# A decayed scan interleaved over chunks, with one gathered reciprocal a chunk, and shorter bias loading one layer later

## What is computed

```python
q = _phi(to_bhtd(q)); k = _phi(to_bhtd(k)); v = to_bhtd(v)   # _phi(x) = elu(x) + 1
kv = k * v
run_kv_f, kv_f1 = _decay_scan(kv, log_a, z)
run_ks_f, ks_f1 = _decay_scan(k, log_a, z)
...
den_f = jnp.clip(jnp.sum(q * run_ks_f, axis=-1, keepdims=True), eps, None)
out_f = (q * run_kv_f / den_f).transpose(0, 2, 1, 3).reshape(B, T, HID)
...
out = jnp.concatenate([out_f, out_s], axis=-1) @ w_out
```

## Time and profile before

| | us |
|---|---|
| median of 3 runs | 3821.74 (3816.81 to 3832.23) |
| the profiled execution, its own time | 3824.2 |
| its span | 3822.5 |
| PE, DVE, ACT, POOL busy | 3128.6, 1936.0, 1324.9, 1112.3 |
| scan stage, from its first DMA to the next stage's | 1841.0 to 2111.1 |
| start of layer 2's attention, its first DMA | 2675.2 |

### The profile page before, as it was taken

The page is one execution under the profiler, slowest core; times in us unless marked ns, Lnnn a source line. Parts: engine busy times, 40 slices in busy tenths (PEclk is TensorE's granted clock), DMA queues, the critical chain, the costliest instruction groups (busy, mean ns, idle before and its releaser), DMA issues. The chain is left out here.

```text
span 3822.5 us, 46802 instructions
## 1 busy us (share of the span) xinstructions
PE 3128.6 (82%) x17066; PEld 1946.8 (51%) x17066; DVE 1936.0 (51%) x3143; ACT 1324.9 (35%) x2216; POOL 1112.3 (29%) x946
## 2 busy tenths in 40 slices
PE   6769999999999899999554874998585667788776
PEld 3445555555555378888322562666463444233354
DVE  3365565565666542332567751111358737466574
ACT  2224444444444343332100541332233414244542
POOL 0015666666666600000111313111342202011231
PEclk9879999999999999999676886999797868589987
DMA  3010000000000011120000134222101000000000
GB/s 105 0 47 1 1 1 1 1 1 1 1 1 1 8 55 50 34 61 28 15 0 0 32 124 134 33 34 43 19 2 30 6 8 2 0 1 1 1 26 25
DMA packets 110925, 89.20 MB, mean 23 GB/s; under 512 B 20451, under 2 KB 104189, under 8 KB 110717
## 3 DMA queue, kind: packets, MB, share of 16 engines
q1 hardware_dynamic: 101501, 75.73, 6.6%
q0 software_dynamic: 7152, 8.55, 1.3%
q10 hardware_dynamic: 2064, 2.10, 0.2%
HBM read 68.32 MB, written 18.94 MB: 23 GB/s over the span
## 5 line engine op out<-in xcount | busy, mean ns | idle before, releaser
L684 POOL TENSOR_TENSOR acc<-acc,pf 128x512 f32<-128x512 f32 (+1 forms) x448 | 563.8, 1280 | 254.4 <-ACT pf L811 254.4
L868 DVE TENSOR_REDUCE mxa<-ps 128x1 f32<-128x512 f32 x512 | 327.3, 681 | 229.2 <-PE ps L730 227.3
L811 ACT ACTIVATE pf<-ps 128x512 f32<-128x512 f32 x512 | 278.0, 595 | 318.7 <-PE ps L705 293.9
L718 PE MATMUL ps<-pf,v 128*64 128x512 f32 (+1 forms) x1152 | 311.0, 618 | 0.0
L3206 DVE TENSOR_REDUCE mx<-ps 128x2 f32<-128x1024 f32 (+1 forms) x192 | 184.0, 958 | 146.7 <-PE ps L3100 108.4
L3194 ACT ACTIVATE pT<-ps 128x1024 f32<-128x1024 f32 (+1 forms) x192 | 153.3, 811 | 207.5 <-PE ps L3112 207.1
L730 PE MATMUL ps<-kH,qH 64*128 64x512 f32 x512 | 158.0, 443 | 23.9 <-DVE mc L876 18.6
L1518 POOL TENSOR_TENSOR e<-e,sm 128x1232 f32<-128x1232 f32 x48 | 107.9, 2248 | 221.6 <-DVE sm L1773 221.6
L1065 POOL TENSOR_TENSOR x<-x,ys 128x256 f32<-128x256 f32 x16 | 11.8, 740 | 508.4 <-DVE ys L1270 508.4
L3096 PE MATMUL ps<-kT,qT 64*128 64x512 f32 (+2 forms) x384 | 98.9, 511 | 66.8 <-DVE mx L3206 59.5
L2165 DVE TENSOR_SCALAR ys<-ps,xs 128x256 f32<-128x256 f32 x39 | 18.8, 483 | 251.4 <-PE ps L2021 251.4
(11 more groups left out here) (498 smaller groups left out, 7169.9 us busy)
## 6 DMA issues: line engine op xcount, KB each, us to landing
w_raw<-in_c_h SPq DMA_DIRECT2D x32, 512.0 KB, 3.8
w1a<-in_f_w SPq DMA_DIRECT2D x8, 1024.0 KB, 15.1
w2a<-in_f_w SPq DMA_DIRECT2D x8, 1024.0 KB, 13.1
moe_rows<-pad SPq DMA_DIRECT2D x1, 5167.5 KB, 19.7
xs<-moe_rows SPq DMA_DIRECT2D x39, 132.5 KB, 2.1
w_raw<-in_c_w SPq DMA_DIRECT2D x32, 128.0 KB, 2.3
x<-in_x SPq DMA_DIRECT2D x1, 2048.0 KB, 8.3
moe_acc<-x ACTq DMA_DIRECT2D x1, 2048.0 KB, 21.1
```

Of the source, the lines that this page charges most:

```text
L684: pool.tensor_tensor(now[0:r, :], now[0:r, :], pf[0:r, n % RING, a, :], ALU.add).then_inc(added.sem, 1)
L718: ins = pe.matmul(g.bk(3)[SIDE[a], :], v[0:r, u // 2 % 2, t, u % 2 * P + a * HD:u % 2 * P + (a + 1) * HD], pf[0:r, n % RING, a, :], start= ...
L811: act.activation(pf[0:r, n % RING, a, :], g.bk(bk.bank[f"s{n}_{a}"])[0:r, :], ACT.Exp, bias=bias)\
L868: dve.tensor_reduce(mxa[:, q % 2, half, a, j:j + 1], g.bk(4 + a), AXX, ALU.max).then_inc(bk.release(f"m{q}_{i}_{a}"), 1)
```

## The change

**Scan stage.** The loops are written out, and the work of three neighbouring chunks is interleaved. PE turns and projects chunk c+1 while DVE scans chunk c and finishes chunk c-1. Features, v and the scans have two buffers each; a scan starts from the last column of the other buffer. The normalisation is part of the block, with z made on ACT (scale `rstd`, shift -mean * rstd). ACT also takes max(x, 0) (`pos`) and copies v out of PSUM, and DVE makes a feature from the two in one pass. The kv product on POOL and the qk product on DVE stay where they were. Denominators are gathered: `summed` has one column per head, 32 for both sets, and four groups of 32 PSUM partitions take the four token tiles, so that one 128x128 tile of bank 4 holds every denominator of a chunk. DVE clamps and inverts this tile alone; PE spreads the inverses back over the features with `spread_back` (16 products a chunk) and DVE multiplies `num` by them, one token tile at a time.

**Layer 2's attention.** The biases come as two rows (`brow`), ACT packs them, four one-column products turn them, ACT copies them to `bcol`. Weights of q and k have a semaphore of their own, and PE starts on them; the wait for the rest comes later.

```diff
@@ -1276,128 +1276,289 @@
...
+        summed, spread_back = sb("summed", [P, NI, 32]), sb("spread_back", [P, NI, P])
...
+        kx, qx, pos = sb("kx", [P, 2, KD, CH]), sb("qx", [P, 2, KD, CH]), sb("pos", [P, 2, KD, CH])
+        v, kv = sb("v", [P, 2, KD, CH]), sb("kv", [P, KD, CH])
+        run_k, run_kv = sb("run_k", [P, 2, NI, CH]), sb("run_kv", [P, 2, NI, CH])
+        qk, num, rec = sb("qk", [P, NI, CH]), sb("num", [P, 2, NI, CH]), sb("rec", [P, P])
...
+            fills += [(f"t0_{c}", 0), (f"t1_{c}", 1), (f"k0_{c}", 2), (f"v0_{c}", 3), (f"q0_{c}", 0), (f"k1_{c}", 1), (f"v1_{c}", 2), (f"q1_{c}", 3)]
+            fills += [(f"d_{c}", 4)] + [(f"b{j}_{c}", 4 + j) for j in range(TC)] + [(f"y{j}_{c}", 4 + j) for j in range(TC)]
...
+                def denominators(c):
+
+                    pe.wait_ge(*bk.free(f"d_{c}", 0))
+                    for n, i in enumerate(ORDER):
+                        pe.wait_ge(*qk_made.at(0, at_scan(i, c)))
+                        for j in range(TC):
+                            ins = pe.matmul(g.bk(4)[32 * j:32 * j + 32, 0:P], summed[:, i, :], qk[:, i, j * P:(j + 1) * P], start=n == 0, stop=n == NI - 1)
+                    ins.then_inc(bk.fill(f"d_{c}"), 1)
+
+                def reciprocals_back(c):
+                    pe.wait_ge(*rec_made.at(0, c + 1))
...
+                        pe.wait_ge(*bk.free(f"b{j}_{c}", 0))
+                    for i in range(NI):
+                        for j in range(TC):
+                            r = slice(32 * j, 32 * j + 32)
+                            ins = pe.matmul(g.bk(4 + j)[:, i * P:(i + 1) * P], spread_back[r, i, :], rec[r, :], start=True, stop=True)
...
+                for c in range(-1, NC + 1):
+                    if 0 <= c - 1:
+                        denominators(c - 1)
+                    if c + 1 < NC:
+                        for n, f in [("t", 0), ("t", 1)] + BLOCKS[0:3]:
+                            if (n, f) == BLOCKS[0]:
+                                pe.wait_ge(*wq_in.at(0, 16))
+                            project(n, f, c + 1)
+                    if 0 <= c - 1:
+                        reciprocals_back(c - 1)
+                    if c + 1 < NC:
+                        for n, f in BLOCKS[3:6]:
+                            project(n, f, c + 1)
+                    if 0 <= c - 1:
+                        output(c - 1)
...
+                    act.activation((kx if n == "k" else qx)[:, h, f, :], src, ACT.Exp).then_inc(ex_made.sem, 1)
+                    act.activation(pos[:, f, n == "q", :], src, ACT.Relu).then_inc(pos_made.sem, 1)
+                    act.wait_ge(*ex_made.at(0, m))
+                    act.wait_ge(*pos_made.at(0, m))
+                    act.sem_inc(bk.release(name), 1)
...
+                for c in range(NC):
+                    for k in range(KD):
+                        act.wait_ge(*bk.full(f"t{k}_{c}", 0))
+                        if c:
+                            act.wait_ge(*bk.full(f"q1_{c - 1}", 0))
+                        act.activation(zT[:, k, :], g.bk(bk.bank[f"t{k}_{c}"]), ACT.Copy).then_inc(bk.release(f"t{k}_{c}"), 1)
+                    if c + 1 < NC:
+                        normalised(c + 1)
+                    for n, f in BLOCKS:
+                        features(n, f, c)
...
+                        pool.wait_ge(*kv_run.at(0, at_scan(i, c)))
+                        if c >= 2:
+                            pool.wait_ge(*bk.full(f"y{TC - 1}_{c - 2}", 0))
+                        pool.tensor_tensor(num[:, h, i, :], qx[:, h, f, :], run_kv[:, h, i, :], ALU.mult).then_inc(num_made.sem, 1)
...
+                    dve.scalar_tensor_tensor(dst, dst, 1.0, pos[:, f, n == "q", :], ALU.min, ALU.add).then_inc(phi.sem, 1)
...
+                    for run, src, made, used in ((run_k, kx[:, h, f, :], k_run, qk_made), (run_kv, kv[:, f, :], kv_run, num_made)):
+                        if c >= 2:
+                            dve.wait_ge(*used.at(0, at_scan(i, c - 2)))
+                        if made is kv_run:
+                            dve.wait_ge(*kv_made.at(0, KD * c + f + 1))
+                        first = none[:, 0:1]
+                        if c % NB:
+                            dve.wait_ge(*made.at(0, at_scan(i, c - 1)))
+                            first = run[:, 1 - h, i, CH - 1:CH]
+                        dve.tensor_tensor_scan(run[:, h, i, :], d, src, first, ALU.mult, ALU.add).then_inc(made.sem, 1)
...
+                    dve.tensor_tensor(qk[:, i, :], qx[:, h, f, :], run_k[:, h, i, :], ALU.mult).then_inc(qk_made.sem, 1)
...
+                    dve.tensor_scalar(rec[:], g.bk(4)[:, 0:P], 1e-6, None, ALU.max).then_inc(bk.release(f"d_{c}"), 1)
+                    dve.wait_ge(*bk.read(f"d_{c}", 0))
+                    dve.reciprocal(rec[:], rec[:]).then_inc(rec_made.sem, 1)
...
+                        dst = num[:, c % 2, :, j * P:(j + 1) * P]
+                        dve.tensor_tensor(dst, dst, g.bk(4 + j).rearrange("p (i n) -> p i n", n=P), ALU.mult).then_inc(y_made.sem, 1)
+                        dve.wait_ge(*y_made.at(0, TC * c + j + 1))
+                        dve.sem_inc(bk.release(f"b{j}_{c}"), 1)
...
+                for c in range(NC + 1):
+                    if c < NC:
+                        made_feature("k", 0, c)
+                        made_feature("q", 0, c)
+                        key_values(0, c)
+                        scans(0, c)
+                        scans(2, c)
+                    if c:
+                        inverted(c - 1)
+                    if c < NC:
+                        made_feature("k", 1, c)
+                        made_feature("q", 1, c)
+                        key_values(1, c)
+                    if c:
+                        divided(c - 1)
+                    if c < NC:
+                        scans(1, c)
+                        scans(3, c)
+                    if c:
+                        added(c - 1)
...
@@ -2254,18 +2417,14 @@
         with nc.Block() as block:
             @block.sync
             def _(sp):
-                for h in range(NH):
-                    f, r = divmod(h, G)
-                    for i, src in enumerate((bk_, bq)):
-                        sp.dma_start(bcol[h % NB * HD:h % NB * HD + HD, 2 * i + h // NB:2 * i + h // NB + 1], src[32 * r:32 * r + HD, f:f + 1],
-                                     allow_slow_non_contiguous=True).then_inc(w_in.sem, 16)
+                for i, src in enumerate((bk_, bq)):
+                    sp.dma_start(brow[0:1, i, :].rearrange("o (f p) -> o f p", p=P), src.rearrange("p f -> f p").unsqueeze(0), allow_slow_non_contiguous=True)\
+                        .then_inc(b_in.sem, 16)
                 for dst, src in ((wk, Wk), (wq, Wq)):
                     for k in range(KD):
                         sp.dma_start(dst[:, k].rearrange("p (h d) -> p h d", d=HD),
-                                     rows(src)[:, k].rearrange("p (h e) -> p h e", e=2 * HD)[:, :, 0:HD]).then_inc(w_in.sem, 16)
-                for dst, src in ((wv, Wv), (wo, Wo)):
-                    load(sp, dst[:], rows(src), w_in)
-                for dst, src in ((rv, bv), (ro, bo), (cau, causal), (same, same_head)):
+                                     rows(src)[:, k].rearrange("p (h e) -> p h e", e=2 * HD)[:, :, 0:HD]).then_inc(kq_in.sem, 16)
+                for dst, src in ((same, same_head), (cau, causal), (wv, rows(Wv)), (rv, bv), (wo, rows(Wo)), (ro, bo)):
...
@@ -2406,11 +2565,16 @@
                         ins = pe.matmul(g.bk(bk.bank[f"w{t}"])[:, 0:D], oT[:, k, :], wo[:, k, :], start=k == 0, stop=k == KD - 1)
                     ins.then_inc(bk.fill(f"w{t}"), 1)
 
+                pe.wait_ge(*bias_dense.at(0, 1))
+                for m in range(2 * KD):
+                    ins = pe.matmul(g.bk(0)[:, m:m + 1], bdense[0:1, m // KD, m % KD * P:(m % KD + 1) * P], g.ident[0:1, 0:1], start=True, stop=True)
+                ins.then_inc(bk.fill("bias"), 1)
+                pe.wait_ge(*kq_in.at(0, 64))
+                for p in start:
+                    project(*p)
                 pe.wait_ge(*made.at(0, 2))
                 pe.wait_ge(*emptied.at(0, 3))
-                pe.wait_ge(*w_in.at(0, 16 * (10 + 2 * NH)))
-                for p in start:
-                    project(*p)
+                pe.wait_ge(*w_in.at(0, 96))
...
+                act.wait_ge(*b_in.at(0, 32))
+                act.activation(bdense[:].rearrange("o i (h d) -> o i h d", d=HD), brow[:].rearrange("o i (h e) -> o i h e", e=2 * HD)[:, :, :, 0:HD], ACT.Copy)\
+                    .then_inc(bias_dense.sem, 1)
+                act.wait_ge(*bk.full("bias", 0))
+                act.activation(bcol[:], g.bk(0)[:, 0:2 * KD], ACT.Copy).then_inc(bk.release("bias"), 1)
+                act.wait_ge(*bk.read("bias", 0))
```

More of the change, by code:

```diff
@@ L1304, in _ @@
             @block.tensor
             def _(pe):
[L1306 to L1314, removed]
-                        for k in range(KD):
[L1316 to L1322, removed]
```

(33 more changed lines are left out.)

216 lines of the change are left out of this document (129 added, 87 removed).

## The result

The changed kernel takes 3684.82 us (median of 4 runs, 3681.95 to 3691.5) where the kernel before takes 3821.18 (4 runs of the same comparison, 3816.81 to 3832.23). The ratio is 0.9641, 95% interval 0.9616 to 0.9667. The forecast was 3665 with a range of 3641 to 3700: the time lies inside it, 20 us above the point.

The account below looks back on a forecast made before the run. The prediction took the scan stage as a DVE-PE chain and layer 2's attention as waiting on SP's DMA queue. Savings of 139.6 and 18.1 us from 3824.2 gave 3666.5, 3665 against the runs' median; range 3641 to 3700.

Parts of the forecast that it names:

- three periods: Scan stage: chunks 1 to 3 each take one period of the fullest queue, DVE, at 25.4 us.
- the 21.8: Scan stage: DVE's own passes, scans, products, denominators and sums in one period, 21.8 us before POOL's effect.
- POOL's charge: Scan stage: DVE loses 0.88 us for each of four POOL products, 3.5 a period, bounds 0 to 5.1.
- A product of DVE took 1.57 us while POOL's ran: Scan stage, kernel before: the next scan began 1.49 us after that product instead of 0.61, so 0.88 lost.
- Rival (b): Scan stage: POOL's products never cost DVE anything, 3651 us, or cost it all, 3680; inside the forecast's 80%.
- rival (a): Scan stage: PE stays at its low clock of 1.2 GHz, 42.2 us a period, total 3715; chance 10%.
- 1 or 2 us late: Scan stage: PE's last output tile may reach DVE 1 or 2 us late in each period; left to the range.
- Rival (d): Scan stage: chunks stay a chain through late buffers or banks, about 36 us a chunk, total 3708; chance 8%.
- The small-packet part of the weights: Layer 2's attention: weights land 7.2 us after first issue, at 2683.6, so PE starts 18.1 us earlier.
- The bound of 5: Layer 2's attention: single-number bias loads on one DMA engine might land 3 to 5 us late; 0 taken.
- Rival (c): Layer 2's attention: 1024 bias packets run serially, losing the whole gain from 0.16 us each; 3862 at 0.2; chance 2%.
- Sum: 139.6 + 18.1 = 157.7: Whole kernel: scan-stage and layer 2 gains added, 157.7 us off the profiled 3824.2, giving 3666.5.

## Why the prediction was nearly right

**Scan stage, right and for the reason given.** Forecast 139.6 less, measured 143.0. Counted from the stage's first DMA, the first projection came after 11.2 us (forecast 11.9), q's feature after 20.0 (21.0), and chunk 0 ended after 38.0 (39.7). The next three chunks start 26.6, 23.8 and 24.5 us apart up to the last inverse, together 75.0 for the 76.2 of three periods; the tail took 13.9 for 14.3. The inverse costs 0.95 + 0.28, a pass of features 0.6, four divisions 3.2 with their waits, a scan 1.2 from start to start: the terms of the 21.8 hold. (With the 3.5 for POOL they make 25.3, not the 25.4 of the forecast.)

**POOL's charge, right in sum, wrong in make-up.** 14 us were charged, 10.4 measured. "A product of DVE took 1.57 us while POOL's ran" was read as a slow `qk`; `qk` is 0.66 in the change. What is lost is 1.0, not 0.88, by the DVE instruction behind the one under way, and ten times, not sixteen: the other six products stand beside the clamp and the inverse or beside the sums, which read one operand from PSUM, and lose nothing. Rival (b) in its first form (never any cost) and in its second (all of 1.27 each) both fall.

**PE's clock, right here.** 0.90, 0.93 and 1.00 in the first three chunks, 0.79 and 0.76 where no projection of another chunk is left; rival (a) fell. DVE's waits for PE at the last tiles of the output, 0.77 and 1.30 in chunk 1, are the "1 or 2 us late" left to the range. Rival (d) fell with the periods.

**Layer 2, right in kind, too large.** The step that failed is "The small-packet part of the weights moved 7881 packets of at most 512 B from 2691.5 to 2697, so they had landed about 7.2 us after the first issue: now 2683.6". It took the weights to move in the change as they had behind the old loads. With two rows of 512 single numbers among them PE starts at 13.1. The bound of 5 was kept for this load, but for its own landing; the landing was on time for PE (7.2 us) and the loss came on the weights behind it. Stage against stage the 18.1 became 13.0. Without the load, 8.95 against 8.5, the term stands. Rival (c) fell: a packet costs 0.009 us, not 0.16.

**The missing 20 us.** The two changed stages together gave 156.0 of 157.7, the scan's surplus and layer 2's shortfall nearly cancelling. The point is off because of the step "Sum: 139.6 + 18.1 = 157.7 from the profiled execution's 3824.2": it took every unchanged stage to stay. In the profiled execution layer 3's block did not, by 24.8 us, at clock 0.75 for 0.83. One kernel showed 421.7 and 390.9 there, so the length is drawn anew in every execution; but the draws with the new scan stage are longer. All unedited stages together took 3325.8 to 3336.5 us in the four profiled executions with the old scan stage, mean 3332.1, and 3336.3 to 3368.2 in the ten with the new one, mean 3353.3. The 21 us between the means are the missing ones. DVE's busy time in these stages is 1643 to 1646 us in all fourteen, so there is no more work; PE's is 2840 to 2850 in the four and 2846 to 2883 in the ten. The timed runs say the same: 3821.18 less 156.0 is 3665.2, and all four runs of the changed kernel, and its fifth, lie above it, by 6.6 to 26.3. Fourteen executions make this likely and don't explain it: why PE runs longer in later, unedited stages behind the new scan stage stays open. Nothing in the forecast's range stood for it; the range was drawn for the rivals, so that the time lies inside it is in part luck.

## What to carry to other kernels

- When GpSimd reads SBUF beside a busy VectorE queue, look at the VectorE instruction *behind* the one under way when GpSimd starts; place the GpSimd work beside VectorE instructions with an operand in PSUM, or beside inverses. Here a mere wait on POOL was worth 6.5 us of DVE.
- A load of many single numbers can cost by what is issued behind it as well as by its own landing: ahead of the weights it made them some 4 us late, behind them its own 7.4 us to landing were waited for. Compare the issue times of the loads behind it, with and without it.
- Before a gain is credited or blamed on a change, cut both traces into stages: what differs in unchanged code is not the edit's own work, here up to 34 us in one block. But repeat both kernels before calling it chance: here all unchanged code together was on average 21 us longer with the new stage.

## What the runs showed that was not expected

- One block of unchanged code, same instruction counts, took 390.9 and 421.7 us in two executions of one kernel; only PE's rows differ, at granted clocks of 0.85 and 0.75.
- SP needed 6.38 us to issue two weight loads that take 2.99 alone, while ACT's queue brought 1024 single numbers.
- A POOL fill of 128x512 (0.52 us) that begins within DVE's `qk` costs DVE nothing, a POOL product of the same tile 1.0 on the scan behind it.
- All unedited stages together took some 21 us longer, on average, in kernels with the new scan stage, by PE's busy time and not by DVE's.
